# Splitting the next head's weights on ScalarE and PoolE instead of ScalarE and VectorE, in an adaLN + gated DeltaNet + sparse FFN block

## What is computed

```python
mod = (silu(c) @ wmod)                                # six modulation rows a sequence: sa, ca, ga, sb, cb, gb
h = layernorm(x) * (1 + ca) + sa
# gated DeltaNet attention, 16 key heads of 128, two value heads of 128 to each
qkv = conv4(h @ W_qkv.T); z = h @ W_z.T               # conv4: causal convolution with four taps
beta = sigmoid(h @ W_b.T); decay = exp(-softplus(h @ W_a.T + dt_bias) * exp(A_log))
q, k = l2norm(q), l2norm(k)
for t in range(256):
    dv = beta_t * (v_t - k_t @ S)
    S = S * decay_t + outer(k_t, dv)
    o_t = q_t @ S
x = x + ga * ((rms_normed(o) * norm_w * silu(z)) @ W_out.T)
# FFN: of four neighbouring hidden values only the two of largest magnitude stay
h = layernorm(x) * (1 + cb) + sb
x = x + gb * (keep_2_of_4(silu(h @ w_gate) * (h @ w_up)) @ w_down)
```

## Time and profile before

| | |
|---|---|
| median of 3 runs | 2099.41 us (2099.03 to 2101.72) |
| the profiled execution: its own time | 2098.93 us |
| its span, first to last instruction | 2097.2 us |
| TensorE matmul busy | 2024.1 us (97%) |
| TensorE weight loads busy (beside the matmuls) | 1673.9 us (80%) |
| VectorE busy | 1870.1 us (89%) |
| ScalarE busy | 1668.9 us (80%) |
| PoolE busy | 1402.2 us (67%) |
| granted TensorE clock, mean | 0.98 |
| HBM traffic | 14 GB/s over the span |

### The profile page before, as it was taken

One profiled execution on the slowest core, in us unless ns is written; L12 is line 12 of the kernel. 1 busy time (PEld: TensorE's weight loads), 2 busy tenths in 40 slices (PEclk: granted clock), 3 DMA queues, 4 the chain that ended last, 5 costly groups with the idle time before them and its releaser, 6 DMA issues.

```text
span 2097.2 us, 61679 instructions
## 1 busy us (share of the span) xinstructions
PE 2024.1 (97%) x23974; PEld 1673.9 (80%) x23974; DVE 1870.1 (89%) x3088; ACT 1668.9 (80%) x3340; POOL 1402.2 (67%) x896
## 2 busy tenths in 40 slices
PE   5599999999999999999999999999999999997999
PEld 3378888888888888888888888888888888886887
DVE  5789999999999999999999999999999999985897
ACT  3488888888888888888888888888888888886332
POOL 3467667777667777667777667777667777663452
PEclk7799999999999999999999999999999999997999
DMA  2000000000000000000000000000000000002100
GB/s 92 21 2 22 2 22 2 22 2 23 2 22 2 2 22 2 22 2 22 2 22 2 22 2 22 2 2 22 2 23 2 22 2 22 2 2 76 41 26 21
DMA packets 12402, 34.06 MB, mean 16 GB/s; under 512 B 1100, under 2 KB 9420, under 8 KB 9684
## 3 DMA queue, kind: packets, MB, share of 16 engines
q1 hardware_dynamic: 12116, 30.11, 4.1%
HBM read 27.99 MB, written 2.11 MB: 14 GB/s over the span
## 4 chain that ended last, share of the span: by engine, by line
PE 93%; DVE 3%; ACT 2%; issue 1%; POOL 1%; DMA 0%; SPq 0%; POOLq 0%; DVEq 0%; ACTq 0%
PE bank L561 83%; PE bank L564 10%; DMA cc<-in_wmod 0%; DVE cc L1596 0%; POOL mask L389 0%; DVE tt L1477 0%; DVE y_acc L1753 0%; DVE yl L1672 0%; ACT sq L1326 0%; ACT sol L1247 0%; DVE w L1572 0%; DVE pt L1646 0%; ACT kn L1175 0%; DVE yl L1503 0%; POOL kx L380 0%
## 5 line engine op out<-in xcount | busy, mean ns | idle before, releaser
L1596 DVE SCALAR_TENSOR_TENSOR cc<-bank,wc,cc 128x510 f32<-128x510 f32 (+2 forms) x768 | 533.9, 736 | 1.1 <-ACT cc L1143 0.8
L561 PE MATMUL bank<-h,w 128*128 128x512 f16 (+1 forms) x1920 | 421.8, 360 | 5.0 <-DVE cc L1596 3.2
L1672 DVE TENSOR_TENSOR yl<-bank,mask 128x512 f16<-128x512 f32 x384 | 263.9, 687 | 53.8 <-PE bank L561 53.8
L437 POOL TENSOR_TENSOR e_b<-ae,b_le 128x1024 f32<-128x1024 f32 x64 | 151.8, 2372 | 214.6 <-ACT ae L1208 214.6
L1224 ACT ACTIVATE inv<-bank 128x512 f16<-128x512 f32 x384 | 231.5, 603 | 74.0 <-PE bank L561 69.0
L561 PEld LDWEIGHTS bank<-h,w 128*128 128x128 f16 x1920 | 172.6, 99 | 144.0 <-issue 4.5
L402 POOL TENSOR_TENSOR g_le<-le,g_cols 128x1024 f16<-128x1024 f16 x128 | 240.8, 1902 | 20.5 <-DVE g_cols L1543 20.5
L1228 ACT ACTIVATE invT<-bank 128x512 f16<-128x512 f32 x384 | 233.1, 607 | 20.8 <-PE bank L561 20.8
L1143 ACT ACTIVATE cc<-bank,wc 128x512 f32<-128x512 f32 x256 | 176.1, 688 | 92.1 <-PE bank L561 92.0
L561 PEld LDWEIGHTS bank<-inv,a 128*128 128x128 f16 x3584 | 187.4, 98 | 58.9 <-ACT inv L1224 17.9
L561 PE MATMUL bank<-inv,a 128*128 128x64 f16 (+1 forms) x3584 | 218.9, 197 | 3.0 <-ACT inv L1224 3.0
(11 more groups left out here) (213 smaller groups left out, 5278.0 us busy)
## 6 DMA issues: line engine op xcount, KB each, us to landing
w_raw<-in_wh SPq DMA_DIRECT2D x16, 1032.0 KB, 4.8
v<-in_x SPq DMA_DIRECT2D x4, 512.0 KB, 4.0
out<-sol SPq DMA_DIRECT2D x16, 128.0 KB, 1.7
w_raw<-in_wgate SPq DMA_DIRECT2D x1, 1024.0 KB, 5.2
cc<-in_wup SPq DMA_DIRECT2D x1, 1024.0 KB, 4.9
pt<-gate_store SPq DMA_DIRECT2D x2, 512.0 KB, 4.5
ae<-in_wdown SPq DMA_DIRECT2D x1, 1024.0 KB, 6.6
sol<-gate_store SPq DMA_DIRECT2D x2, 512.0 KB, 5.9
```

The source lines that it names most:

```text
L437: gp.tensor_tensor(e_b[:, :, 1:P + 1], e_raw, b_le[:], ALU.mult).then_inc(sig("eb"), 1)
L561: return mm(o_, l_, r_, start=start, stop=stop, skip_group_check=True)
L1596: V.scalar_tensor_tensor(dst, src, wc[:, par(s), i, 3 - j:4 - j], dst, ALU.mult, ALU.add).then_inc(sig(f"conv{i}"), 1)
L1672: V.tensor_tensor(lefts(yl[:, l], l), halves(bL[0], l), left(mask[:, l + 1, :], l).unsqueeze(1).broadcast_to([P, U, HP // n_, n_]), ALU.mu ...
```

## The change

ScalarE now does two activations for a quarter: it scales the quarter of `w_raw` in place (f32 to f32), waits for its own result, and copies it to f16 as the high half. PoolE subtracts the high half from the scaled quarter and writes the low half; it does so between `first_inverse` and `decay_operand`. VectorE no longer works on quarters, it only writes the taps in the fourth (now behind a wait for the load, which has long ended there). The rest is bookkeeping: in the FFN part VectorE waits for PoolE's last low half before it writes its own.

```diff
@@ PoolE
+            def split_weights(s):
+
+                if head(s) + 1 >= NK:
+                    return
+                q = blk(s)
+                pool.wait_ge(sig("w_lo"), 4)
+                need(pool, "w_hi", (head(s) + 1) * 4 + q + 1)
+                qs_ = slice(q * 512, q * 512 + 512)
+                gp.tensor_tensor(w16[:, 1 - par(s), 1, qs_], w_raw[:, qs_], w16[:, 1 - par(s), 0, qs_],
+                                 ALU.subtract).then_inc(sig("w_lo"), 1)
+
@@ PoolE, body
                 if s1:
                     first_inverse(s1)
                 if s0:
+                    split_weights(s0)
                     decay_operand(s0)
                     masked_beta(s0)
@@ ScalarE, split_weights
-                A(w16[:, 1 - par(s), 0, q * 512:q * 512 + 512], w_raw[:, q * 512:q * 512 + 512], ACT.Copy,
-                  scale=W_SCALE).then_inc(sig("w_hi"), 1)
+                qs_ = slice(q * 512, q * 512 + 512)
+                A(w_raw[:, qs_], w_raw[:, qs_], ACT.Copy, scale=W_SCALE).then_inc(sig("w_scaled"), 1)
+                act.wait_ge(sig("w_scaled"), head(s) * 4 + q + 1)
+                A(w16[:, 1 - par(s), 0, qs_], w_raw[:, qs_], ACT.Copy).then_inc(sig("w_hi"), 1)
@@ VectorE, split_weights
                 q, n, to = blk(s), N(s), 1 - par(s)
-                need(dve, "w_hi", (head(s) + 1) * 4 + q + 1)
-                qs_ = slice(q * 512, q * 512 + 512)
-                V.scalar_tensor_tensor(w16[:, to, 1, qs_], w_raw[:, qs_], W_SCALE, w16[:, to, 0, qs_], ALU.mult,
-                                       ALU.subtract).then_inc(sig("w_lo"), 1)
                 if q == 3:
+                    need(dve, "w_dma", (head(s) + 2) * 16)
                     need(dve, "tap", (n - q) * 4)
                     tap_weights(to)
@@ VectorE, gate_weights_low
                 dve.wait_ge(sig("w_hi"), NK * 4 + q + 1)
+                dve.wait_ge(sig("w_lo"), NK * 4)
```

## The result

The changed kernel takes 2108.07 us (median of 6 runs, 2107.25 to 2109.2) against 2099.22 us before (6 runs, 2093.93 to 2101.72). The ratio is 1.0048, with an interval of 1.0035 to 1.0061: slower by about 8.9 us. The direction is the forecast one and the time lies in the range; of the forecast 15 us about 60% came.

The account below looks back on a forecast made before the run. TensorE's pace was taken as the bound. PoolE's late `go` costs 0.15 + 0.11 = 0.26 us in 57 steps, 14.8 us; with the first three steps +15 us, forecast 2114 us, range 2107 to 2119.

Parts of the forecast that it names:

- VectorE, 0: Removing VectorE's 60 subtractions gains 0 us: it only waits longer for ScalarE's squares before its sums.
- rival (c): Faster: VectorE, relieved, ends TensorE's 0.14 us wait before `project(3)`; 8 us less, 2091; chance 0.05.
- 0.07 us a step remain at this point: ScalarE's extra activation makes `level_left(5)` 0.21 us late; the wait at `project(3)` absorbs 0.14, leaving 0.07 a step.
- starts 0.05 behind a release: At `level_left(5)`, TensorE was taken to start 0.05 us after ScalarE's `invT` ends.
- 0.15 late: At `turn_output`, the transpose starts 0.15 us late because PoolE's subtraction in front delays `go` by 1.11.
- 0.11 for the exposed weight load: At `turn_output`, TensorE's f32 group pays 0.11 us more after waiting, its first weight load no longer hidden.
- Nothing behind gives it back: After `turn_output`, none of the 0.26 us a step is recovered; other engines start from TensorE's banks until the next `residue`.
- ScalarE's 0.07 under it: ScalarE's 0.07 us is covered by PoolE's 0.26: TensorE reaches `turn_output` 0.07 late and still waits.
- (a): It all fits: `turn_output` has some 0.2 us more room, covering both additions; 0 to 3 us, 2099 to 2102; chance 0.12.
- (b): ScalarE's delay only, PoolE's operation being cheaper at its place: 0.07 to 0.10 us a step, 4 to 6 us; chance 0.12.
- (d): Dearer: delays add, PoolE or ScalarE being late elsewhere; 0.47 us a step, 27 us, 2126; chance 0.08.
- the two signs of being wrong: Prediction wrong if `turn_output` still starts well behind `go`, or if the step grows while `go` is early.

Follow-up runs that it names:

- e5_no_low: Kernel before with no low half computed in the steps by any engine (PoolE clears it once), ScalarE as before; 2099.73 us, ratio 1.0002.
- e4_both_moved: Changed kernel with PoolE's subtraction behind `scaled_output`, ScalarE's scaling behind `inverse_right(5)` and its copy behind `refined`; 2099.0 us, ratio 0.9996.
- e1_act_only: Changed kernel with the subtraction back at VectorE's old place; ScalarE keeps scaling and copy, PoolE does nothing for the weights; 2108.46 us, ratio 1.0044.
- e3_pool_behind_go: Changed kernel with PoolE's subtraction moved behind `scaled_output`, so that `go` is as early as before; 2109.01 us, ratio 1.0042.
- e9_xt_first: As e3_pool_behind_go, with the two waits of `level_left` turned (`xt_ready` written before `ym`); 2103.32 us, ratio 1.0016.
- e6_pool_twice: Changed kernel with a second, identical subtraction on PoolE that waits for the first; 2175.4 us (one run).
- e2_pool_only: Changed kernel with ScalarE making one activation a quarter as before; PoolE subtracts at the change's place, from the unscaled quarter; 2104.79 us, ratio 1.0026.
- e10_both_first: Changed kernel with the order of waits turned in `level_left` and at `turn_output`; 2104.38 us, ratio 1.0026.

## Why the prediction was right, and where not

**VectorE, 0: right.** `e5_no_low` and `e4_both_moved` show it directly, and the last four steps are 28.56 in the changed kernel too. The idle time came to 0.75 us, forecast 0.8, but 0.49 of it already at `keys_low`, which waits for ScalarE, and not before the sums. What the prediction quotes with rival (c) from the Trainium skill's Perfetto Trace Analysis page (§ Identifying the Most-Contended Engine), to optimise the engine with the highest occupancy first, which is VectorE by its count, has no support in any of the runs: VectorE makes no low half in any kernel but `e1_act_only`, and none of them is faster than before.

**"0.07 us a step remain at this point": the term that failed.** It measured 0.17 (`e1_act_only`, `e3_pool_behind_go`). Every duration in it was right within 0.02, the self wait and the 0.14 given back at `project(3)` too (0.13). What was wrong is "starts 0.05 behind a release". I had taken that 0.05 from the residue, whose late wait is written first; in `level_left(5)` the late one is written last and stands apart, which is 0.15. `e9_xt_first` brings it back to 0.05.

**"0.15 late", and "0.11 for the exposed weight load", 0.26 in all: wrong in three pieces.** `go` moved by 1.12 (forecast 1.11). The release was 0.15 here as well, which makes the wait 0.26 when PoolE's part is alone. Against that, the exposed weight load was read rightly for `sol,pt` (in the kept trace the second product of 1012.76 starts 0.21 us behind the first, the others 0.11 apart, and at 1017.97 all are 0.11 apart), but it doesn't carry over to transposes that wait in an instruction apart: there it is 0.03. And "Nothing behind gives it back" was wrong: 0.16 us come back between `turn_output` and `level_rows(1)`, with a wait of 0.26 and with the 1.32 of `e6_pool_twice`. In the kernel before, two more waits lie there, which a late `go` covers. The fifth transpose starts 0.14 us behind the fourth and the sixth 0.17 behind the fifth instead of 0.11, as the fifth needs VectorE's last convolution of the values (over at 1014.17, its weight load starts at 1014.23). Of these 0.09 us the 0.03 above go off, and 0.06 come back. The other 0.10 are at `sol,kx`, which needs ScalarE's copy `o`:

```profile
1014.00 0.66 ACT L1260 ACTIVATE o<-bank 128x512 f32<-128x512 f32 x1
```

```profile
1014.71 0.73 PEld L561 LDWEIGHTS bank<-sol,kx 128*128 128x128 f32 x4
```

`o` is over at 1014.66, and the first weight load comes 0.05 behind it with nothing left to hide it: the second of the four products starts 0.32 us behind the first, the rest are 0.22 apart. In `e2_pool_only` `o` is over 0.15 us before that load (1017.66 and 1017.81), and all four products are 0.22 apart. 0.26 was forecast, 0.11 is the part alone, and in the change it is 0.

**"ScalarE's 0.07 under it": the mechanism is right**, two delays of one chain of TensorE cover each other and the longer counts (0.17 and 0.11 make 0.17, 0.03 and 0.11 make 0.11, 0.17 and 1.34 make 1.34). Only which is the longer was the wrong way round.

**The rivals.** (a) falls: neither part fits. (b) named the true mechanism, "ScalarE's delay only", but for the reason that PoolE's operation is cheaper at its place, which it isn't, and at half the price. (c) falls as said. (d), delays that add, falls with `e6_pool_twice` and with the change itself.

**The signs** that were named: steps of 28.8 (28.73) and 28.56 at the end came true; `level_left(5)` 0.2 later was 0.31; the wait of `project(3)` is gone. `go` ends 0.15 and not 0.05 before its transposes, and these did not take 0.1 longer. Of the two signs of being wrong the second came true: in `e1_act_only` and `e3_pool_behind_go` `go` is early, and the step grows by the full 0.17 all the same. The total of +15 was near enough since the forecast's largest term, too large by 0.15, hid a term too small by 0.10. It was the right direction partly by luck: had the release been 0.05 as assumed and the 0.16 come back, the same working would have given 0.07 us a step, 4 us, at the edge of what can be measured. `e10_both_first` is nearly that kernel, and measured 0.10 us a step and 5.6 us.

## What to carry to other kernels

Cost the two ends of a wait separately: how late the producer is, and how the consumer is released, for which the neighbouring row must have its late wait at the same place among its waits. Look behind a late start as well as ahead of it: the short waits that follow it are covered by it, and what they cost before is given back, once. Before moving work between engines to relieve one, look for a stretch of the same trace in which that work is missing already; it priced the relief at nothing, and the place on the receiving engine (`e4_both_moved` against the change) decided all of the loss.

## What the hardware showed that I had not expected

- A TensorE group with more waits than one starts 0.15 us behind the end of what it waits for if the late one is written last, 0.05 to 0.06 if it is written first: both ways round at two places (1010.77 to 1010.92 and 1020.69 to 1020.84 in the change, 1009.35 to 1009.40 in `e9_xt_first`, 988.85 to 988.91 in `e10_both_first`). Not all of the 0.10 is gained: 0.03 go again between the first and the second transpose (0.17 us instead of 0.14), 0.01 to 0.02 in the products behind `level_left(5)`, and one turned pair shortened the step by 0.07 (`e9_xt_first`). Where the other wait is the late one, the turned order costs instead: 0.06 us in `level_left(1)`, which here came back at the decay products.
- An activation that waits for the one just ahead of it starts 0.03 us behind its end, but 0.13 us later than without the wait (0.65 in the mean of the steps against 0.52, from start to start), since two independent ones overlap by 0.10.
- On PoolE the same is 1.24 against 1.12 us, 0.12 for a wait for its own result.
- A group of TensorE that starts right behind the end of what it waited for is late twice: its first weight load is not hidden, and its second matmul comes 0.10 us later than the pace of the others in the f32 products (`sol,pt` 0.21 instead of 0.11, `sol,kx` 0.32 instead of 0.22), 0.03 to 0.06 in f32 transposes.
- Not settled: the first `go` of the profiled executions starts at 154.12 us before, 156.90 after, 152.54 in `e3_pool_behind_go` and 156.35 in `e9_xt_first`, though their code up to there is nearly the same. It is why spans were not compared.
